# Local attention: the blocks of the transposed weights in another order, so that constant zero columns are neither copied nor multiplied

## The chip, the cores and the metric

One core of a Trainium2 chip runs the whole program. The metric is the device time of one execution in microseconds (us); below it stands the median of several executions. TensorE multiplies (PE in the profile, its weight loads PEld), VectorE (DVE), ScalarE (ACT) and GpSimd (POOL) work beside it, and SyncE (SP) issues transfers.

## What is computed

Six blocks are applied one after the other to x of shape 4 x 256 x 256 (batch, tokens, features), each with a residual: cross attention over 4096 context tokens, causal attention with a convolution, a local transformer of six layers, a second cross attention, gated linear attention and a mixture of experts. The change acts on the third, and rearranges the second. Each layer of the third has 16 heads of 64 features and attends inside a window:

```
def local_attention(q, k, v):            # n = 256 tokens, WINDOW = 64
    ...
    mask = (it < jb) | (it > jb + w) | (jb == -1)
    sim = jnp.einsum('bhwie,bhwje->bhwij', bq, bk2) * QK_SCALE
    sim = jnp.where(mask, -jnp.finfo(sim.dtype).max, sim)
    attn = jax.nn.softmax(sim, -1)
    out = jnp.einsum('bhwij,bhwje->bhwie', attn, bv2)
```

So token i sees the tokens i-64 to i. Tokens 192 to 255 see none of the tokens 0 to 127.

## The kernel before

The six blocks run in turn, each as one stage with a program for each engine. Local (L1365 on) is the stage of the local transformer. It has 24 jobs, one for each layer l and batch b, and a plan that is written out by hand: TABLE and LOADS give each step a tick, a job has 24 ticks, and all steps are sorted by tick. Every engine walks through this one sorted plan in order, so that an engine that waits holds up everything that it has behind the wait. The attention of a job is laid over the projections of the next one (HEADS = 24.18 ticks later): projections (L1911, 128x512 passes in fp32r), rotary embedding on VectorE (L1775 to L1779), the squares on ScalarE (L1686), transposes of q and k (L1948), then the heads, the output projection (L1976), a normalisation (L1836 to L1856), the transposes of its result (L1989), the feed-forward's matmuls (L1998 and L2008). At the change of a layer, the next layer's projection weights are split into a high and a low part by ScalarE (L1679) and VectorE (L1748).

The heads are the work of the class Attention, which the second block (Conv) uses too. A head n passes through four kinds of steps, and every step comes to all engines:

- front: two score matmuls (L1017). Query tile 0 (tokens 0 to 127) meets keys 0 to 127, and query tile 1 (tokens 128 to 255) meets keys 64 to 255, 192 of them, because the constructor gets skip = 64. VectorE adds the mask and takes the smallest value (L1053), and ScalarE takes the exponential (L1078). Both write p, 384 columns wide: columns 0 to 127 are query tile 0, columns 128 to 191 are zeros that were set once, columns 192 to 383 are query tile 1 on keys 64 to 255.
- divide: the reciprocal of the sum (L1058), and the products on VectorE (L1061) and GpSimd (L1068).
- turn: three transposes of 128x128 (L1026) into one PSUM bank, and one copy of 384 columns to pt by ScalarE (L1084). The blocks of pt are, in order: queries 0 to 127 on keys 0 to 127; queries 128 to 255 on keys 0 to 127; queries 128 to 255 on keys 128 to 255. In the second block the columns of queries 192 to 255 are zeros.
- apply: for two heads at once (at_once = 2, one in the rows 0 to 63 of the PSUM bank and one in the rows 64 to 127), the values of the first key tile times 256 columns of pt, then the values of the second key tile times 128 columns, added to the right half (L1037). Each of these float32 matmuls appears in the trace as two passes, so that an apply is 8 passes. ScalarE copies the result away (L1530).

Over the 24 jobs there are 384 heads and 192 applies. In Conv skip is 0 and at_once is 4; there are 128 heads there.

Of the kernel before, what the change touches and what calls it, by code (L numbers as in the profile page):

```python
# [7 lines left out]
F32 = mybir.dt.float32  # L8
# [5 lines left out]
P = 128  # L14
# [11 lines left out]
class Flow:  # L26


    def __init__(self, sem, step):
        self.sem, self.step, self.base, self.n = sem, step, 0, 0  # L30
# [934 lines left out]
class Attention:  # L965
# [8 lines left out]
    def __init__(self, c, name, ctx, banks, n_pt, at_once, rounds, skip):  # L974
        nc = c.nc
        self.c, self.at_once, self.rounds = c, at_once, rounds
        self.s_banks, self.t_banks, self.o_bank = banks
        self.keys, self.first, self.off = (P, 2 * P - skip), (0, skip), (0, P)
        self.place = (0, P + skip)
        self.width, self.n_pt, self.step = sum(self.keys), n_pt, P // at_once  # L980
        self.p = ctx.enter_context(nc.sbuf_tensor(f"{name}_p", [P, 5, 3 * P], F32))
        self.pt = ctx.enter_context(nc.sbuf_tensor(f"{name}_pt", [P, n_pt, 3 * P], F32))
        self.stat = ctx.enter_context(nc.sbuf_tensor(f"{name}_stat", [P, 5, 4, 2], F32))
        f = c.flow
        self.s_full, self.low_done, self.exp_done = f("at_s_full"), f("at_low_done"), f("at_exp_done")
        self.div_dve, self.div_pool = f("at_div_dve"), f("at_div_pool")
        self.t_full, self.t_out = f("at_t_full"), f("at_t_out")
        self.pv_done, self.o_out = f("at_pv_done"), f("at_o_out")
# [21 lines left out]
    def pe_step(self, pe, on, st, step):  # L1010
        kind, n, b, h = step
        NS = len(self.s_banks)
        if kind == "front":
            s = self.s_banks[n % NS]
            on.wait_ge(self.low_done, 2 * (n - NS) + 2)
            for q in range(2):
                mm = pe.matmul(s[:, self.off[q]:self.off[q] + self.keys[q]], st.q_of(b, h, q),  # L1017
                               st.k_of(b, h, self.first[q], self.keys[q]), start=True, stop=True)
            mm.then_inc(*self.s_full.one())
        elif kind == "turn":  # L1020
            on.wait_ge(self.div_dve, 2 * n + 2)
            on.wait_ge(self.div_pool, n + 1)
            on.wait_ge(self.t_out, n - 1)
            for i in range(3):
                at = slice(i * P, (i + 1) * P)
                tr = pe.transpose(self.t_banks[n % 2][:, at], self.p[:, n % 5, at], self.c.ident[:, :])  # L1026
            tr.then_inc(*self.t_full.one())
        elif kind == "apply":
            heads, call = h, n // self.at_once
            round_ = call % self.rounds  # L1030
            on.wait_ge(self.t_out, n + len(heads))
            if round_ == 0:
                on.wait_ge(self.o_out, call // self.rounds)
            for first, cols, keys, kt in ((True, slice(0, 2 * P), slice(0, 2 * P), 0),
                                          (False, slice(P, 2 * P), slice(2 * P, 3 * P), 1)):
                for j, head in enumerate(heads):
                    mm = pe.matmul(self.o_bank[self.step * j:self.step * j + self.step, cols],  # L1037
                                   st.v_of(b, kt, head), self.pt[:, (n + j) % self.n_pt, keys],
                                   start=first and round_ == 0,
                                   stop=not first and round_ == self.rounds - 1)  # L1040
            mm.then_inc(*self.pv_done.one())

    def dve_step(self, dve, on, st, step):
# [27 lines left out]
    def act_step(self, act, on, st, step):  # L1071
        kind, n, b, h = step
        t3 = self.stat[:, n % 5, :, :]
        if kind == "front":
            for q in range(2):
                low = self.p[:, n % 5, self.place[q]:self.place[q] + self.keys[q]]
                on.wait_ge(self.low_done, 2 * n + q + 1)
                act.activation(low, low, ACT.Exp, bias=t3[:, 0, q:q + 1], scale=-1.0,  # L1078
                               accum_out=t3[:, 2, q:q + 1]).then_inc(*self.exp_done.one())
        elif kind == "turn":  # L1080
            on.wait_ge(self.t_full, n + 1)
            if n >= self.n_pt:
                on.wait_ge(self.pv_done, (n - self.n_pt) // self.at_once + 1)
            act.activation(self.pt[:, n % self.n_pt, :], self.t_banks[n % 2][:, 0:3 * P],  # L1084
                           ACT.Copy).then_inc(*self.t_out.one())
        elif kind == "apply":
            call = n // self.at_once
            if call % self.rounds == self.rounds - 1:
                on.wait_ge(self.pv_done, call + 1)
                st.keep(act, on, n, b, h, self.o_bank)  # L1090
# [2049 lines left out]
```

## Time and profile before

| | |
|---|---|
| median of 3 runs | 4458.15 us (4455.14 to 4465.23) |
| profiled execution | 4470.84 us |
| its span in the trace | 4469.0 us |
| mean granted TensorE clock | 0.968 |
| stage of the local transformer | about 1290 to 2965 us of the span |

The profiled execution is one execution of its own and lies 12.7 us above the median. The trace gives, for each engine, when each instruction began and how long it took; matmuls overlap in their pipeline, so their durations add up to more than the time that they hold TensorE.

### The profile page before, as it was taken

What the parts mean: (1) busy time and instruction counts of PE and PEld (TensorE: products, weight loads), DVE (VectorE), ACT (ScalarE), POOL (GpSimd) and SP (SyncE); (2) the same over time, 40 slices, a digit from 0 to 9 for tenths busy, and PEclk for the clock granted to TensorE, in tenths of its full rate; (3) what the DMA queues carried; (4) which work ended last, traced back from release to release, by engine and by line L of the source; (5) the groups of instructions that cost most, each with busy time, mean ns of one, the idle gap of its engine ahead of it and who ended that gap; (6) DMA issues with size and microseconds to landing.
All of it is one profiled execution on the core that took longest, in us unless ns stands there. A gap on an engine that the chain in (4) does not pass through costs nothing. (4 is left out here: it accounts for less than half of the span.)

```text
span 4469.0 us, 83297 instructions
## 1 busy us (share of the span) xinstructions
PE 4072.7 (91%) x30320; PEld 2916.0 (65%) x30320; DVE 3121.6 (70%) x7923; ACT 2814.7 (63%) x5769; POOL 1809.5 (40%) x1862
## 2 busy tenths in 40 slices
PE   6899999898979999999999999968999999977898
PEld 4555555555757888888878888845555555545677
DVE  5677777776777767667677676546777777767645
ACT  3666666667976777777677676715666666654322
POOL 3322222212566565555556555413223222201544
PEclk8999999999989999999999999989999999988999
DMA  6655556545020100001100101036556555512265
GB/s 153 133 105 108 103 98 115 109 64 203 10 76 5 34 31 30 24 29 32 39 22 25 38 22 38 15 84 138 114 101 111 102 106 106 100 27 70 83 177 190
DMA packets 208206, 354.14 MB, mean 79 GB/s; under 512 B 26927, under 2 KB 110564, under 8 KB 205745
## 3 DMA queue, kind: packets, MB, share of 16 engines
q1 hardware_dynamic: 200217, 338.42, 34.0%
q0 software_dynamic: 7584, 10.39, 0.7%
q8 instruction: 246, 4.03, 0.4%
q14 instruction: 159, 1.30, 0.1%
HBM read 257.48 MB, written 114.98 MB: 83 GB/s over the span
## 5 line engine op out<-in xcount | busy, mean ns | idle before, releaser
L754 DVE TENSOR_REDUCE xa_m_part<-xa_ring 128x1 f32<-128x512 f32 x2048 | 1318.4, 685 | 501.6 <-PE xa_ring L907 487.1
L676 ACT ACTIVATE xa_ex<-xa_sc 128x1024 f32<-128x1024 f32 x1024 | 991.4, 1022 | 120.6 <-PE xa_sc L893 105.4
L907 PE MATMUL xa_ring<-xa_ks,xa_q_base 48*128 48x512 f32 x2048 | 521.4, 500 | 166.9 <-DVE xa_m_part L754 131.6
L921 PE MATMUL xa_pv<-xa_ex,xa_vs 128*17 128x256 f32 x8192 | 553.1, 388 | 1.7 <-issue 1.7
L1068 POOL TENSOR_SCALAR lt_p<-lt_p,lt_stat 128x192 f32<-128x192 f32 x384 | 354.6, 924 | 456.0 <-DVE lt_stat L1058 455.4
L907 PEld LDWEIGHTS xa_ring<-xa_ks,xa_q_base 48*128 48x128 f32 x2048 | 202.6, 186 | 497.5 <-DVE xa_m_part L754 431.0
L1911 PE MATMUL lt_bank<-lt_wp,lt_xt 128*128 128x512 f32 x1728 | 465.6, 411 | 13.6 <-DVE lt_wp L1748 6.0
L893 PE MATMUL xa_sc<-xa_q_base,xa_ks 50*128 50x256 f32 x4096 | 423.7, 302 | 27.9 <-ACT xa_k L648 4.5
L893 PEld LDWEIGHTS xa_sc<-xa_q_base,xa_ks 50*128 50x128 f32 x4096 | 347.7, 188 | 122.3 <-ACT xa_vs L663 24.6
L1078 ACT ACTIVATE lt_p<-lt_p,lt_stat 128x128 f32<-128x128 f32 (+1 forms) x768 | 321.8, 420 | 157.4 <-DVE lt_stat L1053 154.8
L1911 PEld LDWEIGHTS lt_bank<-lt_wp,lt_xt 128*128 128x128 f32 x1728 | 315.2, 192 | 78.7 <-DVE lt_xt L1741 9.1
L1625 POOL TENSOR_TENSOR lt_r_qk<-lt_r_qk,lt_t_rot 128x512 f32<-128x512 f32 x192 | 267.5, 1394 | 203.9 <-DVE lt_t_rot L1779 198.2
L1053 DVE CUSTOM_DVE_ANT_0 lt_p<-lt_bank,lt_mask,lt_rq 128x128 f32<-128x128 f32 (+1 forms) x768 | 260.9, 376 | 123.7 <-PE lt_bank L1017 120.6
L598 POOL CAST xa_kp<-xa_k 128x512 fp32r<-128x512 f32 (+1 forms) x144 | 86.2, 599 | 625.2 <-ACT xa_k L656 286.7
L921 PEld LDWEIGHTS xa_pv<-xa_ex,xa_vs 128*17 128x17 f32 x8192 | 189.7, 97 | 201.3 <-issue 63.7
L1632 POOL TENSOR_TENSOR lt_nrm<-lt_nrm,minus_half 128x16 f32<-128x16 f32 x96 | 281.9, 2936 | 21.6 <-DVE lt_nrm L1796 18.7
L1998 PE MATMUL lt_bank<-lt_ft,lt_w 128*128 128x256 f32 x1152 | 267.7, 383 | 9.3 <-DVE lt_ft L1856 5.9
L1686 ACT ACTIVATE lt_t_sq<-lt_bank 128x512 f32<-128x512 f32 x192 | 114.7, 598 | 226.2 <-DVE lt_t_rot L1779 226.2
L1998 PEld LDWEIGHTS lt_bank<-lt_ft,lt_w 128*128 128x128 f32 x1152 | 214.7, 191 | 41.5 <-issue 12.6
L610 POOL TENSOR_SCALAR xa_m_neg<-xa_m_blk 128x8 f32<-128x8 f32 x128 | 29.7, 232 | 520.1 <-DVE xa_m_blk L765 515.1
L876 PE MATMUL xa_sc<-xa_wp,xa_cxp 128*128 128x256 f32 x1536 | 213.7, 289 | 0.0
L862 PE MATMUL xa_sc<-xa_cxp,xa_wp 128*128 128x512 f32 x744 | 211.4, 421 | 0.0
(325 smaller groups left out, 7943.0 us busy)
## 6 DMA issues: line engine op xcount, KB each, us to landing
xa_ks<-keys SPq DMA_DIRECT2D x372, 256.0 KB
keys<-xa_kp SPq DMA_DIRECT2D x128, 512.0 KB, 3.8
xa_cx<-in_ctx_t SPq DMA_DIRECT2D x64, 512.0 KB
lt_u<-in_lt_wqkv SPq DMA_DIRECT2D x54, 256.0 KB
places<-in_moe_blank SPq DMA_DIRECT2D x47, 258.0 KB, 9.6
moe_xs<-places SPq DMA_DIRECT2D x47, 258.0 KB
lt_w<-in_lt_w SPq DMA_DIRECT2D x6, 1536.0 KB
xa_q_base<-xa_m_rows SPq DMA_DIRECT2D x512, 2.0 KB
```

What stands on the lines that cost most here:

```text
L676: act.activation(x.ex[:, n % x.NE, :, :], x.sc[n % 2][:, :, :], ACT.Exp).then_inc(*x.ex_done.one())
L754: dve.tensor_reduce(x.m_part[:, i % 2, qt, h, ch:ch + 1], x.bank(n + odd), AX.X, ALU.max).then_inc(*x.dve_out.one())
L893: mm = pe.matmul(x.sc[n % 2][:, 2 * odd + pair, :], x.ks[unit % x.NU][rows, 2 * (g % 2) + pair, kt * P:(kt + 1) * P], x.q_base[rows, 2 * g ...
L907: pe.matmul(x.bank(n + odd), x.q_base[rows, pair, b * S + qt * P:b * S + (qt + 1) * P], x.ks[unit % x.NU][rows, pair % 4, ch * 512:(ch + 1 ...
L921: mm = pe.matmul(x.pv[32 * j:32 * j + x.VW, :], x.vs[:, i % x.NV, kt, 4 * g + j, :], x.ex[:, n % x.NE, 2 * (j % 2) + j // 2, :], start=(kt ...
L1053: dve.tensor_tensor_reduce(self.p[:, n % 5, to], s[:, at], st.mask[:, at], st.minus_scale(b, h, q), -NEG, ALU.add, ALU.min, t3[:, 0, q:q + ...
L1068: pool.tensor_scalar(sv, sv, self.stat[:, n % 5, 3, 1:2], None, ALU.mult).then_inc(*self.div_pool.one())
L1078: act.activation(low, low, ACT.Exp, bias=t3[:, 0, q:q + 1], scale=-1.0, accum_out=t3[:, 2, q:q + 1]).then_inc(*self.exp_done.one())
L1625: pool.tensor_tensor(out, out, self.t_rot[:, t, :], ALU.add).then_inc(*self.rot_add.one())
L1632: pool.tensor_tensor(n[:, 2, :], n[:, 1, :], c.minus_half[:, 0:H], ALU.pow).then_inc(*self.rnorm.one())
L1911: mm = pe.matmul(bank[:, :], self.xt[:, par, xpart, k, tile * P:(tile + 1) * P], self.wp[:, wpart, sec, k, half * 512:half * 512 + 512], s ...
L1998: mm = pe.matmul(bank[:, gate * S:(gate + 1) * S], self.w1[:, k, gate * FFP + m * P:gate * FFP + (m + 1) * P], self.ft[:, k, :], start=(k ...
```

## The change

The three transposes write to other places of their PSUM bank. The block of queries 128 to 255 on keys 128 to 255 comes first, that of queries 0 to 127 on keys 0 to 127 second, and that of queries 128 to 255 on keys 0 to 127 last, so that the 64 columns of zeros lie at the end. The copy to pt ends ahead of them (320 columns in place of 384), and the matmul on the first key tile takes the 192 columns that are left in place of 256. The output columns 192 to 255 are then written for the first time by the matmul on the second key tile, which has start=False. In Conv the widths stay as they were and only the order of the blocks is another.

```
+        self.both, self.whole = 2 * P - skip, skip == 0
-        self.pt = ctx.enter_context(nc.sbuf_tensor(f"{name}_pt", [P, n_pt, 3 * P], F32))
+        self.pt = ctx.enter_context(nc.sbuf_tensor(f"{name}_pt", [P, n_pt, 3 * P - skip], F32))
...
-            for i in range(3):
-                at = slice(i * P, (i + 1) * P)
-                tr = pe.transpose(self.t_banks[n % 2][:, at], self.p[:, n % 5, at], self.c.ident[:, :])
+            for i, to in enumerate((P, 2 * P, 0)):
+                tr = pe.transpose(self.t_banks[n % 2][:, to:to + P], self.p[:, n % 5, i * P:(i + 1) * P],
+                                  self.c.ident[:, :])
...
-            for first, cols, keys, kt in ((True, slice(0, 2 * P), slice(0, 2 * P), 0),
-                                          (False, slice(P, 2 * P), slice(2 * P, 3 * P), 1)):
+            for first, cols, keys, kt in ((True, slice(0, self.both), slice(P, P + self.both), 0),
+                                          (False, slice(P, 2 * P), slice(0, P), 1)):
...
-                                   stop=not first and round_ == self.rounds - 1)
+                                   stop=not first and round_ == self.rounds - 1,
+                                   skip_group_check=not self.whole)
...
-            act.activation(self.pt[:, n % self.n_pt, :], self.t_banks[n % 2][:, 0:3 * P],
+            act.activation(self.pt[:, n % self.n_pt, :], self.t_banks[n % 2][:, 0:self.width],
                            ACT.Copy).then_inc(*self.t_out.one())
```

## Rows read from the trace of the kernel before

**Rows 1.** The page's busy time of each engine over the whole span.
```profile
PE 4072.7 (91%) x30320; PEld 2916.0 (65%) x30320; DVE 3121.6 (70%) x7923; ACT 2814.7 (63%) x5769; POOL 1809.5 (40%) x1862
```

**Rows 2.** Busy time of each engine in the stage, then in its steady part.
```profile
core 0: us, PE busy (x) PEld busy (x) DVE busy (x) ACT busy (x) POOL busy (x), PEclk, DMA share, GB/s
1290.00:2965.00 1675.00, 1611.37 (x9479) 1335.81 (x9480) 1143.59 (x3899) 1164.85 (x3073) 933.15 (x747) 0.98 0.10 31
1345.00:2920.00 1575.00, 1542.62 (x9210) 1282.83 (x9211) 1083.20 (x3763) 1129.76 (x3019) 902.44 (x727) 1.00 0.09 27
```

**Rows 3.** Who waited for whom, 1345 to 2920 us: total, times, longest (us).
```profile
DVE lt_p L1053 <- PE lt_bank L1017: 116.5, 82, 3.9
DVE lt_r_qk L1775 <- PE lt_bank L1911: 78.2, 80, 2.2
...
PE lt_bank L1948 <- DVE lt_r_qk L1805: 14.6, 7, 2.7
...
PE lt_bank L1998 <- DVE lt_ft L1856: 4.8, 15, 0.6
PE lt_bank L1998 <- issue: 3.4, 6, 0.6
...
PEld lt_bank L1037 <- ACT lt_pt L1084: 1.5, 3, 0.8
```

**Rows 4.** Groups by line and shape, 1345 to 2920 us: busy us, mean ns.
```profile
L1084 ACT ACTIVATE lt_pt<-lt_bank 128x384 f32<-128x384 f32 x384 | 183.1, 477 | 1.8
L1037 PE MATMUL lt_bank<-lt_pt,lt_v 128*64 128x256 f32 x768 | 125.3, 405 | 0.8 <-ACT lt_pt L1084 0.8
L1017 PE MATMUL lt_bank<-lt_kt,lt_q_odd 128*128 128x192 f32 x382 | 95.1, 331 | 0.0
L1037 PE MATMUL lt_bank<-lt_pt,lt_v 128*64 128x128 f32 x768 | 74.6, 273 | 0.0
L1530 ACT ACTIVATE lt_ot<-lt_bank 128x256 f32<-128x256 f32 x192 | 69.7, 363 | 1.0 <-PE lt_bank L1037 1.0
```

**Rows 5.** Timeline of TensorE around one apply: start us, us.
```profile
1902.56 0.60 PE L1948 MATMUL lt_bank<-ident,lt_r_qk 128*128 128x128 f32 x4
1903.00 0.71 PE L1017 MATMUL lt_bank<-lt_kt,lt_q_odd 128*128 128x128 f32 x4
1903.55 0.49 PE L1026 MATMUL lt_bank<-ident,lt_p 128*128 128x128 f32 x3
...
1904.52 0.87 PE L1037 MATMUL lt_bank<-lt_pt,lt_v 128*64 128x256 f32 x8
1905.32 0.33 PE L1026 MATMUL lt_bank<-ident,lt_p 128*128 128x128 f32 x1
```

**Rows 6.** Timeline of TensorE, one long run of 256-column passes.
```profile
2923.07 7.07 PE L1976 MATMUL lt_bank<-lt_wo,lt_ot 128*128 128x256 f32 x32
```

**Rows 7.** Timelines of VectorE and TensorE ahead of a job's first L1998.
```profile
1638.79 0.69 DVE L1775 TENSOR_TENSOR lt_r_qk<-lt_bank,lt_tab 128x512 f32<-128x512 f32 x1 [1.48 <-PE lt_bank L1911]
...
1642.78 0.98 DVE L1856 TENSOR_SCALAR lt_ft<-lt_bank,lt_lnc 128x256 f32<-128x256 f32 x2
...
1641.95 0.87 PE L1037 MATMUL lt_bank<-lt_pt,lt_v 128*64 128x256 f32 x8
...
1643.91 3.69 PE L1998 MATMUL lt_bank<-lt_ft,lt_w 128*128 128x256 f32 x16 [0.61 <-DVE lt_ft L1856]
```

**Rows 8.** The same two engines where a layer ends.
```profile
2297.40 0.69 DVE L1775 TENSOR_TENSOR lt_r_qk<-lt_bank,lt_tab 128x512 f32<-128x512 f32 x1 [1.06 <-PE lt_bank L1911]
...
2317.18 2.98 DVE L1748 TENSOR_TENSOR lt_wp<-lt_u,lt_wp 128x512 fp32r<-128x512 f32 x3 [0.28 <-ACT lt_wp L1679]
...
2315.53 0.87 PE L1037 MATMUL lt_bank<-lt_pt,lt_v 128*64 128x256 f32 x8
...
2322.95 0.66 PE L1948 MATMUL lt_bank<-ident,lt_r_qk 128*128 128x128 f32 x4 [2.21 <-DVE lt_r_qk L1805]
```

**Rows 9.** VectorE and the others between the first and last row above.
```profile
2297.40:2322.95 25.55, 22.60 (x136) 17.87 (x135) 24.96 (x74) 19.56 (x54) 18.58 (x14) 1.00 0.14 44
```

**Rows 10.** Windows of 14 us at two layers' ends (PEclk is the clock's share).
```profile
1777.00:1791.00 14.00, 11.63 (x58) 9.84 (x57) 8.75 (x24) 9.80 (x23) 4.30 (x4) 0.88 0.01 2
2317.00:2331.00 14.00, 11.16 (x63) 9.11 (x64) 9.64 (x27) 10.61 (x28) 4.85 (x5) 1.00 0.01 1
```

**Rows 11.** The same wait of TensorE at three more layers' ends.
```profile
1783.09 0.93 PE L1948 MATMUL lt_bank<-ident,lt_r_qk 128*128 128x128 f32 x4 [2.19 <-DVE lt_r_qk L1805]
2053.04 1.12 PE L1948 MATMUL lt_bank<-ident,lt_r_qk 128*128 128x128 f32 x4 [2.22 <-DVE lt_r_qk L1805]
2592.05 0.92 PE L1948 MATMUL lt_bank<-ident,lt_r_qk 128*128 128x128 f32 x4 [2.20 <-DVE lt_r_qk L1805]
```

## The prediction

> **What bounds the kernel now.** I read the page's busy times first: TensorE is busy for 91% of the span, VectorE for 70%, ScalarE for 63% [rows 1]. Those are means over six stages with different limits, so the next view is the windows. The change touches only the stage of the local transformer, 1290 to 2965 us. In its steady part, 1345 to 2920 us, TensorE is busy for 1542.6 of 1575 us (98%), at a granted clock of 1.00, while ScalarE has 1129.8 us of work (72%), VectorE 1083.2 (69%) and GpSimd 902.4 (57%) [rows 2]. Durations of matmuls overlap, so 98% could still hide pauses. The waits settle that: the largest that TensorE has for another engine is 14.6 us, for the scaled keys, then 4.8 and 3.4 us at the first matmul of the feed-forward. VectorE waits for TensorE 116.5 us at the scores and 78.2 us at the projections [rows 3]. TensorE sets the pace and the others follow it. So the question is what the change takes out of TensorE's stream, and how much of that TensorE then spends waiting.
>
> **The wide matmuls of apply.** An apply has 8 passes of TensorE: 4 of 256 columns and 4 of 128, 768 of each over the stage [rows 4], which are 192 applies. Durations say little about how long a pass holds the engine; starts do. 32 passes of 256 columns take 7.07 us from the first start to the last end. The last alone lasts about 0.38 us, so there are 31 steps in 6.69 us, 216 ns each [rows 6]. Passes of 128 columns start every 0.44 / 4 = 110 ns. The scores, two of 128 and two of 192, take 1903.55 - 1903.00 = 0.55 us, which leaves (0.55 - 0.22) / 2 = 165 ns for one of 192 [rows 5]. So 256 to 192 columns is worth 216 - 165 = 51 ns; by the lengths of the same passes it is (405 - 273) / 2 = 66 ns for 64 columns, where 405 holds a start-up share that won't shrink, and by the spacing of 256 and 128 it is (216 - 110) / 2 = 53 ns. I take 53.
>
> The two heads go to different rows of the bank. One apply takes 1905.32 - 1904.52 = 0.80 us up to the next transposes [rows 5]; four 256-column and four 128-column passes one after the other would take 1.3 us. So the two heads' passes run side by side, and the 8 passes are 4 pairs, of which 2 are narrowed. The saving is 2 x 53 = 106 ns for an apply and 192 x 0.106 = 20.4 us for the stage. The other two pairs, the start-up and the step back to full-width transposes stay as they are. No pass is added. That the last 64 output columns are first written by a matmul with start=False costs nothing that I can find: it has the same columns and the same number of passes. No row shows such a write; between 0 and a step of 110 ns for an apply (the nearest pass) it could cost 0 to 21 us, and I take 0, since it replaces a write of the same size to the same bank.
>
> The Trainium skill (TensorE: Matmul & The Clock Gate, "Back-to-back issue gap") puts the spacing of warm matmuls at columns / 2.4 plus 2.5 ns, which would be 109 ns for 256 columns. The trace has twice that for these float32 passes [rows 6], and the trace decides. By the page 64 columns are worth 27 ns, and the sum above would be an estimated 10.2 us.
>
> **The copy.** The copy to pt takes 477 ns for 384 columns, and ScalarE's copy of 256 columns out of the same kind of bank takes 363 [rows 4]: 0.89 ns for a column, 57 ns for 64. Over 384 heads ScalarE gets 21.9 us back, of its 1129.8. It has 28% idle, and TensorE waited for pt for 1.5 us in all [rows 3], because the apply comes several steps after the turn in the plan. I cost it at nothing; the cover is TensorE's own work between turn and apply. The upper bound is what TensorE's waits on it hold, 1.5 us, and if more of the late scores hang on ScalarE's queue, about as much again: 3 us.
>
> **The order of the transposes.** Three transposes of the same size into the same bank, and the copy waits for the last one either way: 0. In Conv the widths are unchanged too, so 0 for its 128 heads. The buffer pt gets smaller, and no transfer or wait is added or moved.
>
> **What is given back in waits.** The shortening acts where TensorE leads. Where VectorE leads over a stretch, TensorE only comes earlier to a wait that ends at the same time. There are two such places.
> - Ahead of each job's first L1998. VectorE last waited for TensorE at 1638.79 us. From there it works without a pause to L1856 at 1642.78, whose end lets TensorE go on at 1643.91 after 0.61 us of waiting. One apply, at 1641.95, lies within [rows 7]. That saving of 0.106 us is lost. The wait shows 15 + 6 = 21 times [rows 3]: 2.2 us.
> - Where a layer ends. VectorE has the splits of the next weights on top: from 2297.40 to 2322.95 us it is busy for 24.96 of 25.55 us, and TensorE waits 2.21 us at the end of it [rows 8, 9]. In this stretch I count three applies, of which the last, at 2315.53, belongs to the first place. Two more by 0.106 us by five ends of a layer: 1.1 us.
>
> What is late next: steps that now have less slack than up to 0.9 us a job (8 applies by 0.106) will begin to show as waits. The rows don't give the slack; the bounds are 0 and, if every job had one more such place with half its applies ahead of it, 24 x 0.4 = 10 us. VectorE is idle for 31% of the time and mostly waits for TensorE, so I stay near the low end, 1 us.
>
> **Sum.** 20.4 - 2.2 - 1.1 - 1.0 = 16.1 us. The profiled execution took 4470.8 us and should come to 4454.7. It lies 12.7 us above the median of the runs; I take the same saving off the median: 4458.2 - 16.1 = 4442 us. About 0.2% (9 us) is what a measurement of this kernel can tell from no change.
>
> **The rivals.**
> - *The forecast* (0.67): TensorE keeps the lead, 13 to 20 us are saved, 4438 to 4445 us.
> - *More* (0.10): ScalarE's shorter queue brings scores and tiles forward where TensorE waited. To 20.4 come the 3 us above: 4435 us. For it: ScalarE is the second busiest engine. Against: almost no wait of TensorE ends on it [rows 3].
> - *A narrower pass gives less than its columns* (0.09): by the page's gap, named above, or because the pass in each apply that loads its weights uncovered hides part of the stream. With half the saving on the pairs, 20.4 / 2 = 10.2, less half of the 3.3 given back: 8.6 us, 4450 us. Against it: the scores' 192 columns at 165 ns [rows 5], a like pass of full width.
> - *Given back in waits* (0.10): the 10 us bound holds rather than 1. 20.4 - 3.3 - 10 = 7 us, 4451 us; with VectorE leading for more of the job, down to nothing, 4458. For it: VectorE had no slack in the stretch of rows 9. Against: outside such stretches it waits for TensorE in each job [rows 3].
> - *Slower, by the clock* (0.04): after some ends of a layer the clock is halved for a while; the window from 1777 us has 0.88 of it, so (1 - 0.88) x 14 / 0.5 = 3.4 us at 1.2 GHz, while that from 2317 us has 1.00 [rows 10]. TensorE had waited 2.2 us before both. Layers with the fall last 269.95 us (1783.09 to 2053.04), one without 269.10 (2322.95 to 2592.05) [rows 8, 11], so a fall costs 0.85 us there, and 1.7 us (half of 3.4) in a stretch without slack. If longer waits brought it in after each of the 21 + 5 waits, that is 26 x 1.7 = 44 us against 16 saved: 28 us slower, 4486 us. It decides from about 15 more falls on, as 25 us would be needed to be 0.2% slower. Against it: the waits grow by only 0.1 to 0.3 us, and 0.6 us waits leave the clock at 1.00 now.
>
> **How the numbers follow.** The forecast and *more* are faster by over 0.2%, and so is near half of *a narrower pass gives less*, as 8.6 us is just under the 9 us bound: 0.67 + 0.10 + 0.04 = 0.81, plus 0.01 of the waits. The rest of these two is no change: 0.14. Slower keeps 0.04. The range goes from *more* with the spread of a median, 4432, to the upper bounds of the two small-gain cases, 4452; what it leaves out is most of the waits case below 6 us and the clock.
>
> **What would show it.** Right: L1037's wide passes listed as 128x192, near 330 ns; an apply that takes 0.69 us in place of 0.80; the copy as 128x320 near 420 ns; ScalarE's busy time in the stage down by 22 us; the job's period down by 0.6 to 0.8 us; TensorE's waits at L1998 and L1948 larger by 3 to 4 us in all; all other stages unchanged. Wrong: an apply that still takes 0.75 us or more (a pass is worth less than its columns), or an apply of 0.69 us with waits of TensorE that grew by 10 us or more (VectorE leads), or windows with a clock under 1.00 inside jobs (the clock).

## The result and the profile after

The changed kernel takes 4444.5 us (median of 20 runs, 4427.9 to 4459.0), the kernel before 4459.7 us (20 runs, 4450.3 to 4470.5). The ratio is 0.9965, with an interval of 0.9955 to 0.9974: 15.6 us faster, between 11.6 and 20.1 (the medians are 15.2 us apart). The forecast was 16.1 us. On two more chips the changed kernel came out at 0.996 (0.9946 to 0.9974) and 0.9964 (0.995 to 0.9979) of the kernel before.

The page of the changed kernel, its busy times, beside [rows 1]:

```profile
PE 4047.2 (91%) x30320; PEld 2906.1 (65%) x30320; DVE 3123.8 (70%) x7923; ACT 2795.1 (63%) x5769; POOL 1811.3 (41%) x1862
```

The same number of instructions, 25.5 us less on TensorE, 19.6 us less on ScalarE, VectorE and GpSimd as before. The windows of the stage in the changed kernel, its whole length and its steady part (us, busy and count for each engine, TensorE's clock, DMA), answer to [rows 2]:

```profile
core 0: us, PE busy (x) PEld busy (x) DVE busy (x) ACT busy (x) POOL busy (x), PEclk, DMA share, GB/s
1297.50:2945.80 1648.30, 1581.17 (x9458) 1326.21 (x9459) 1138.83 (x3883) 1142.37 (x3069) 933.05 (x745) 0.99 0.10 31
1351.00:2907.00 1556.00, 1518.13 (x9214) 1276.44 (x9213) 1084.82 (x3765) 1110.08 (x3020) 903.75 (x727) 1.00 0.09 28
```

and the window of the same length of work in the kernel before, from the stage's first matmul to its last:

```profile
1291.40:2958.90 1667.50, 1607.52 (x9459) 1333.49 (x9460) 1137.68 (x3882) 1162.29 (x3068) 931.75 (x745) 0.98 0.10 31
```

The stage is 19.2 us shorter. TensorE is still busy for 98% of the steady part, so it is still the bound. The spans of the two profiled executions differ by more, 4469.0 to 4443.8 = 25.2 us. From its first matmul to its last, the stage of the experts took 383.1 us in the one and 370.8 in the other, and the first cross attention 1035.6 and 1041.4, with the same instructions: that part is not the change's. The experts' stage takes from 369.4 to 383.1 us in ten of the fourteen profiles, with the change and without it.

The groups by line and shape in the steady part of the changed kernel (busy us, mean ns), beside [rows 4]:

```profile
L1086 ACT ACTIVATE lt_pt<-lt_bank 128x320 f32<-128x320 f32 x384 | 162.8, 424 | 1.8
L1038 PE MATMUL lt_bank<-lt_pt,lt_v 128*64 128x192 f32 x768 | 104.8, 352 | 0.6 <-ACT lt_pt L1086 0.5
L1038 PE MATMUL lt_bank<-lt_pt,lt_v 128*64 128x128 f32 x768 | 74.6, 273 | 0.0
L1532 ACT ACTIVATE lt_ot<-lt_bank 128x256 f32<-128x256 f32 x192 | 69.7, 363 | 0.9 <-PE lt_bank L1038 0.9
```

The wide passes went from 405 to 352 ns, 53 less; the passes of 128 columns stayed at 273 ns and the copy of the result at 363. The copy went from 477 to 424 ns. TensorE's timeline of the changed kernel where [rows 7] were read:

```profile
1644.63 0.76 PE L1038 MATMUL lt_bank<-lt_pt,lt_v 128*64 128x192 f32 x8
1645.33 0.55 PE L1026 MATMUL lt_bank<-ident,lt_p 128*128 128x128 f32 x3
1646.60 3.69 PE L2000 MATMUL lt_bank<-lt_ft,lt_w 128*128 128x256 f32 x16 [0.72 <-DVE lt_ft L1858]
```

An apply takes 1645.33 - 1644.63 = 0.70 us in place of 0.80 [rows 5]. Over all 192 applies the median from an apply's first start to the next pass behind it went from 802 to 695 ns, 107 less. The wait behind the apply shown is 0.72 us in place of 0.61 [rows 7]: what this apply saved, TensorE waits.

Three waits in the steady part (total us, times, longest), first of the kernel before, then of the changed one: TensorE's for the low part of the features (lt_xt), its wait for the gate of the feed-forward (lt_u), and that of its weight loads ahead of the feed-forward:

```profile
PE lt_bank L1911 <- DVE lt_xt L1741: 2.8, 5, 0.6
PE lt_bank L1948 <- DVE lt_u L1869: 2.3, 3, 1.2
...
PEld lt_bank L1998 <- issue: 12.6, 21, 0.8
```

```profile
PE lt_bank L1913 <- DVE lt_xt L1743: 4.0, 5, 0.8
PE lt_bank L1950 <- DVE lt_u L1871: 3.8, 6, 1.2
...
PEld lt_bank L2000 <- issue: 14.9, 21, 0.9
```

Last, the wait at two layers' ends in the changed kernel, beside [rows 11], and windows of 14 us at them, beside [rows 10]:

```profile
1784.55 0.66 PE L1950 MATMUL lt_bank<-ident,lt_r_qk 128*128 128x128 f32 x4 [2.22 <-DVE lt_r_qk L1807]
2051.06 0.66 PE L1950 MATMUL lt_bank<-ident,lt_r_qk 128*128 128x128 f32 x4 [2.22 <-DVE lt_r_qk L1807]
```

```profile
1780.00:1794.00 14.00, 11.26 (x66) 9.26 (x65) 8.72 (x28) 10.54 (x26) 4.65 (x4) 1.00 0.01 2
2313.00:2327.00 14.00, 11.26 (x67) 9.24 (x66) 8.79 (x28) 10.54 (x26) 4.64 (x5) 1.00 0.00 1
```

A layer takes 2051.06 - 1784.55 = 266.5 us. In the kernel before it was 269.1 with the full clock and 269.95 with a stretch at the half clock [rows 8, 11]. So the change is worth 2.6 us a layer, and the clock's fall, which this execution doesn't show at any layer's end, 0.85 us. The stage has six layers, so an estimate of the change's own part of it is 6 x 2.6 = 15.6 us. That this is the figure of the timed runs to the tenth is chance, as their interval reaches about 4 us to each side. The rest of the 19.2 us goes with the clock: the execution before has such stretches at three layers' ends and one in the first layer, the one after none. Each lasts 3.4 us.

### The profile page after: what moved, and what is told of

Same layout as the page of the kernel before. It is cut to its first block and busy times, and to the rows that moved or that the text cites. A ratio compares the mean times of both kernels' runs of the same rounds, so it can differ in the third digit from the quotient of the medians.

```text
span 4443.8 us, 83297 instructions
## 1 busy us (share of the span) xinstructions
PE 4047.2 (91%) x30320; PEld 2906.1 (65%) x30320; DVE 3123.8 (70%) x7923; ACT 2795.1 (63%) x5769; POOL 1811.3 (41%) x1862
## 5 line engine op out<-in xcount | busy, mean ns | idle before, releaser
L2000 PE MATMUL lt_bank<-lt_ft,lt_w 128*128 128x256 f32 x1152 | 267.2, 382 | 11.6 <-DVE lt_ft L1858 7.5
L2000 PEld LDWEIGHTS lt_bank<-lt_ft,lt_w 128*128 128x128 f32 x1152 | 214.3, 191 | 43.7 <-issue 14.9
```

Source lines behind the costliest of these rows:

```text
L2000: mm = pe.matmul(bank[:, gate * S:(gate + 1) * S], self.w1[:, k, gate * FFP + m * P:gate * FFP + (m + 1) * P], self.ft[:, k, :], start=(k ...
```

## The experiments

Theory A: TensorE's stream sets the pace, so the gain is the columns of the wide passes, less what is lost in waits where VectorE leads. The rivals are that the order of the blocks (B) or ScalarE's shorter copy (C) gives a part of it, that a pass has a floor or VectorE soon takes the lead (D), and two on the waits (E) and on the array's rows (F, G).

Single timed runs of one kernel scatter by 9 to 31 us, and the runs came in three groups, each on one chip, with the kernel before at 4466.8, 4435.1 and 4458.1 us (chips 1 to 3 below). So each run's profile is read for two lengths that the rest of the kernel doesn't touch: the stage, from its first matmul to its last, and one layer, from a layer's first apply to the next layer's (the second to the fifth were read). "Falls" counts the stretches at the half clock in the stage's steady part, the first layer included. The edits below are against the changed kernel, that of before_ft_first against the kernel before; lines are shortened with "...".

| kernel | ratio to before (interval) | stage us | falls | layer us, without / with a fall |
|---|---|---|---|---|
| before (profile of the prediction) | 1 | 1667.6 | 4 | 269.1 / 269.9 |
| changed (profile of the result) | 0.9965 (0.9955 to 0.9974) | 1648.4 | 0 | 266.5 / - |
| after_again, chip 1 | 0.996 (0.9946 to 0.9974) | 1651.0 | 3 | 266.5 / 267.3 |
| order_only, chip 1 | 1.0003 (0.999 to 1.0016) | 1667.8 | 4 | 269.1 / 270.0 |
| copy_only, chip 1 | 0.9998 (0.9987 to 1.0009) | 1667.7 | 4 | 269.1 / 269.9 |
| mm_only, chip 1 | 0.9957 (0.9945 to 0.997) | 1650.7 | 2 | 266.6 / - |
| mm_128, chip 2 | 0.9928 (0.9908 to 0.9948) | 1638.2 | 4 | 264.0 / 265.0 |
| ft_first, chip 2 | 0.9933 (0.9913 to 0.9953) | 1646.1 | 5 | - / 266.2 |
| before_ft_first, chip 2 | 0.9991 (0.9976 to 1.0005) | 1659.9 | 4 | 267.8 / 268.7 |
| half_rows, chip 2 | 1.0135 (1.0114 to 1.0157) | 1729.4 | 4 | 279.7 / 280.8 |
| after_2, chip 3 | 0.9964 (0.995 to 0.9979) | 1650.8 | 2 | 266.5 / - |
| ft_first_2, chip 3 | 0.9952 (0.9939 to 0.9966) | 1644.1 | 5 | - / 266.0 |
| splits_late, chip 3 | 0.9956 (0.9944 to 0.9969) | 1652.5 | 2 | 266.1 / - |
| ft_splits, chip 3 | 0.9958 (0.9943 to 0.9972) | 1647.0 | 6 | - / 266.2 |

### The change itself again: after_again and after_2

> The changed kernel as it is, beside the others on one chip. Both theories expect what the study's result gave: ratio 0.9965, about 15 to 16 us under the kernel before.

> The changed kernel once more, beside the three below on one chip: ratio about 0.996 to the kernel before, 32 applies (one layer) in 266.5 us where the clock stays full and 267.4 where it is halved for a while.

The layers are the same to 0.1 us in all three profiles where the clock stays full. A fall at a layer's end adds 0.8 us (267.3 and 266.5), and between 0.8 and 1.1 us in the other kernels of the table. Two of them in the stage's first layer add 2.5 us (259.1 in both of these profiles, 256.6 in that of the result, which has none).

### One part at a time: order_only, copy_only, mm_only

> Only the order of the blocks of the transposed weights is changed; the copy stays at 384 columns and the wide passes at 256. Theory A (TensorE's stream sets the pace, and only its columns count): no change, within 3 us of the kernel before; an apply still takes 0.80 us. Rival B (part of the gain comes from the new places of the blocks in the banks): 3 to 8 us faster.

```
-        self.both, self.whole = 2 * P - skip, skip == 0
+        self.both, self.whole = 2 * P, True
-        self.pt = ... [P, n_pt, 3 * P - skip]
+        self.pt = ... [P, n_pt, 3 * P]
-            act.activation(self.pt[...], self.t_banks[n % 2][:, 0:self.width], ...)
+            act.activation(self.pt[...], self.t_banks[n % 2][:, 0:3 * P], ...)
```

No change: 1.0003, and the stage is within 0.2 us of that before, with as many falls. Rival B is out.

> New order, copy of 320 columns, passes still 256 wide (the last 64 columns of the buffer are set to zero once). ScalarE gets about 21 us of work less. Theory A: 0 to 2 us faster, because TensorE hardly ever waits for ScalarE. Rival C (ScalarE, the second busiest engine, shares the pace): 5 to 10 us faster, a third to a half of the gain.

```
-        self.both, self.whole = 2 * P - skip, skip == 0
+        self.both, self.whole = 2 * P, True
-        self.pt = ... [P, n_pt, 3 * P - skip]
+        self.pt = ... [P, n_pt, 3 * P]
-            act.activation(self.pt[:, n % self.n_pt, :], ...)
+            act.activation(self.pt[:, n % self.n_pt, 0:self.width], ...)
+                dve.memset(self.at.pt[:, :, 3 * P - WINDOW:3 * P], 0.0)
```

The groups of copy_only show the two halves apart, the short copy and the wide passes:

```profile
L1086 ACT ACTIVATE lt_pt<-lt_bank 128x320 f32<-128x320 f32 x380 | 161.2, 424 | 1.8
L1038 PE MATMUL lt_bank<-lt_pt,lt_v 128*64 128x256 f32 x760 | 124.0, 405 | 0.1
```

ScalarE has its 53 ns a head, and the stage is as long as before: 1667.7 us, ratio 0.9998. The copy is worth nothing here. The interval of the ratio alone reaches to 5.8 us faster; it is the stage that rules rival C out.

> New order, passes 192 wide, copy still of 384 columns. Theory A: the whole gain, 14 to 17 us faster than the kernel before, within 2 us of the changed kernel. Rival C: 5 to 10 us short of it. The apply should take 0.69 us in place of 0.80 either way.

```
-        self.pt = ... [P, n_pt, 3 * P - skip]
+        self.pt = ... [P, n_pt, 3 * P]
-            act.activation(self.pt[...], self.t_banks[n % 2][:, 0:self.width], ...)
+            act.activation(self.pt[...], self.t_banks[n % 2][:, 0:3 * P], ...)
```

The groups of mm_only:

```profile
L1086 ACT ACTIVATE lt_pt<-lt_bank 128x384 f32<-128x384 f32 x384 | 183.5, 478 | 1.8
L1038 PE MATMUL lt_bank<-lt_pt,lt_v 128*64 128x192 f32 x768 | 104.8, 352 | 0.8 <-ACT lt_pt L1086 0.8
```

0.9957, and a layer of 266.6 us against 266.5 of the whole change. All of the gain is the narrow passes: the applies of mm_only take 695 ns, as in the changed kernel, and those of copy_only 802, as before.

One row needs care. The weight loads of apply seem to wait for the copy much more in the changed kernel than in mm_only. Waits of TensorE's weight loads (total us, times, longest), the changed kernel:

```profile
PEld lt_bank L1038 <- issue: 33.0, 146, 0.3
...
PEld lt_bank L1038 <- ACT lt_pt L1086: 11.1, 46, 0.8
```

In the kernel before, and in mm_only, the same two read 42.7 and 1.5 us; in copy_only they read 33.2 and 10.8. The sums are 44.1, 44.2, 44.2 and 44.0: the pause ahead of an apply is the same, and only its label moves when the copy is shorter.

### The same step once more: mm_128

> The changed kernel with the first key tile's passes 128 wide in place of 192; it leaves out the products of queries 128 to 191 with keys 0 to 127. Theory A (time goes by columns, less what is given back where VectorE leads): the same step once more, another 13 to 16 us, 28 to 32 us faster than the kernel before, an apply of 0.58 us, and TensorE's wait ahead of each job's first feed-forward matmul 0.1 us longer again. Rival D (passes have a floor set by their weight loads or VectorE takes the lead): under 8 us more than the change gave.

```
-        self.both, self.whole = 2 * P - skip, skip == 0
+        self.both, self.whole = 2 * P - 2 * skip, skip == 0
```

This kernel leaves out products that the result needs; it is there for its time alone. TensorE's timeline of mm_128 at the same place:

```profile
1637.69 0.66 PE L1038 MATMUL lt_bank<-lt_pt,lt_v 128*64 128x128 f32 x8
1638.28 0.55 PE L1026 MATMUL lt_bank<-ident,lt_p 128*128 128x128 f32 x3
1639.70 3.69 PE L2000 MATMUL lt_bank<-lt_ft,lt_w 128*128 128x256 f32 x16 [0.87 <-DVE lt_ft L1858]
```

An apply takes 0.59 us (median 588 ns, again 107 less), the wait 0.87, and a layer 264.0 us: 2.5 us less again, where 32 applies by 0.106 would be 3.4. Six layers make that 15 us; the ratio, 0.9928, says about 16 us more than the change's 0.9965, within wide intervals. The step repeats with nearly the same loss, so down to passes of 128 columns there is no floor and rival D is out.

### Who leads ahead of the feed-forward: ft_first and before_ft_first

> The changed kernel with one step of the plan moved: the second half of the first projection comes behind the transposes of the normalised features instead of ahead of them, so that VectorE's scaling of them isn't behind three rotary operations and TensorE has six passes to do meanwhile. Theory A (VectorE's queue order makes the wait of 0.34 to 0.9 us in nearly every job, and a part of the saving is lost in it): the wait ahead of the first feed-forward matmul goes, and the kernel gains 8 to 14 us over the changed one. Rival E (the wait only moves to the next step behind VectorE): under 4 us.

> The kernel before with the same step moved. Theory A: 6 to 11 us faster than the kernel before (its waits there are 2 us shorter in all than in the changed kernel), so that narrow passes on top of it are worth 17 to 19 us in place of 15.5, since that apply's saving isn't lost. Rival E: no change, and narrow passes are worth 15 to 16 us as before.

```
-    TABLE = ((-5.23, "proj", 0, 0, 0), (-4.15, "proj", 0, 0, 1), ...
+    TABLE = ((-5.23, "proj", 0, 0, 0), (-3.4, "proj", 0, 0, 1), ...
```

The ratios, 0.9933 and 0.9991, would make the narrow passes worth 26 us on top of the moved step. The profiles contradict that: a layer is 267.8 us without a fall, and 266.2 with one, so about 265.35 without (by 0.85 for a fall): 2.45 us, not more than the 2.6 of the unmoved plan. Where both have a fall it is 268.7 against 266.2, again 2.5 us. Theory A had expected the narrow passes to be worth more there; they aren't, and rival E had that right. On the moved step itself it was right by the profile: a layer takes 267.8 us in place of 269.1, and the stage, with four falls in each, 7.7 us less. The timed runs, 4 us with an interval that reaches from 11 us faster to 2 slower, don't settle that. Next, ft_first beside the changed kernel on one chip.

> ft_first once more, now on the same chip as the changed kernel. From its profile (a layer in 266.2 us with the halved clock at each layer's end, against 266.5 without it in the changed kernel) the theory now is that the moved step gains 1.2 us a layer and a longer wait at the layer's end takes 0.85 back through the clock: 2 to 7 us faster than the changed kernel. Rival: the 12 us that the ratios of different chips seemed to show.

TensorE's timeline of ft_first_2, ahead of the feed-forward and at a layer's end:

```profile
1635.83 0.55 PE L1026 MATMUL lt_bank<-ident,lt_p 128*128 128x128 f32 x3
1636.21 3.62 PE L2000 MATMUL lt_bank<-lt_ft,lt_w 128*128 128x256 f32 x16
...
1641.36 0.66 PE L1950 MATMUL lt_bank<-ident,lt_r_qk 128*128 128x128 f32 x4 [0.16 <-DVE lt_u L1871]
```

```profile
1774.10 1.02 PE L1950 MATMUL lt_bank<-ident,lt_r_qk 128*128 128x128 f32 x4 [2.84 <-DVE lt_r_qk L1807]
...
2040.10 0.79 PE L1950 MATMUL lt_bank<-ident,lt_r_qk 128*128 128x128 f32 x4 [2.84 <-DVE lt_r_qk L1807]
```

and its windows at two layers' ends:

```profile
1771.00:1785.00 14.00, 11.16 (x61) 9.69 (x60) 7.19 (x26) 10.78 (x26) 5.20 (x4) 0.88 0.01 2
2037.00:2051.00 14.00, 11.16 (x62) 9.66 (x61) 7.18 (x26) 10.83 (x27) 5.25 (x4) 0.88 0.01 1
```

The wait ahead of L2000 is gone, as theory A had it, so VectorE's order of work did cause it. But a wait of 0.16 us stands five microseconds later, that at the layer's end grew from 2.22 to 2.84 us (VectorE itself now waits 1.18 us there for ScalarE's part of the splits, L1681, in place of 0.28), and the clock now falls at four of the five layers' ends (all five in ft_first). A layer takes 266.0 us in place of 266.5. On the one chip the medians are 4438.4 and 4441.7 us, with ratios whose intervals overlap. Those 3 us are in line with the second expectation, and far from the 8 to 14 us of the first; there rival E was nearer. The 12 us between the ratios of chips 1 and 2 didn't come again, and the stages show no such difference.

### Who leads where a layer ends: splits_late and ft_splits

> The changed kernel with VectorE's four splits of the next layer's key weights (2.8 us) behind the scaling of the keys instead of ahead of it. Theory A (the queue order of VectorE makes the wait of 2.4 us at each layer's end, and what narrow passes save in that stretch is lost there): the wait falls under 0.8 us, a layer takes 264.5 to 265.5 us, no halved clock, 5 to 9 us faster than the changed kernel. Rival (the splits only move the wait behind themselves, to the gates of the feed-forward): a layer still takes over 266 us.

```
-             (20.73, "split", 3, (1, 0)), (20.85, "split", 3, (1, 1)), ...
+             (21.4, "split", 3, (1, 0)), (21.5, "split", 3, (1, 1)), ...
```

TensorE's timeline of splits_late where a layer ends:

```profile
2315.64 0.60 PE L1950 MATMUL lt_bank<-ident,lt_r_qk 128*128 128x128 f32 x4
...
2319.72 0.66 PE L1950 MATMUL lt_bank<-ident,lt_r_qk 128*128 128x128 f32 x4 [2.60 <-DVE lt_u L1871]
```

The first transposes no longer wait, the next ones wait 2.60 us, now for the gate of the feed-forward (L1871). A layer is 266.1 us, so the rival was right that the wait moves. But VectorE's queue isn't what holds the gate. VectorE's timeline of splits_late, the last split and the gate:

```profile
2316.57 0.68 DVE L1750 TENSOR_TENSOR lt_wp<-lt_gl,lt_wp 128x512 fp32r<-128x512 f32 x1
2317.17 0.67 DVE L1791 TENSOR_REDUCE lt_nrm<-lt_t_sq 128x8 f32<-128x512 f32 x1
2319.18 0.88 DVE L1871 SCALAR_TENSOR_TENSOR lt_u<-lt_bank,lt_ffc,lt_gl 128x256 f32<-128x256 f32 x2 [1.34 <-ACT lt_gl L1721]
```

VectorE is idle for 1.34 us ahead of the gate, at each of the five layers' ends, and waits for ScalarE, whose own step (L1721) waits in the program for the splits (L1715). ScalarE begins it at 2317.31, 0.06 us after the last split has ended, with a table load of 1.28 us, and only then computes what the gate needs. So the chain that took over is split, ScalarE's table load and gate, VectorE's gate. No run takes the table load out of it.

> Both moves of the plan in the changed kernel. Theory A: the two places where VectorE leads are both relieved, a layer takes 263 to 264.5 us, 10 to 16 us faster than the changed kernel, about 0.993 of the kernel before. Rival (a third place takes over): under 8 us.

Both moves together give 266.2 us a layer with a fall in each, a stage of 1647.0 us and a ratio of 0.9958. That is no better than ft_first_2 alone, and the rival was right. TensorE waits 3.15 us for the gate at each layer's end, and ahead of it VectorE waits for ScalarE as in splits_late (1.34 us at each of the five ends). No version that computes the same is clearly faster than the changed kernel in the timed runs; by its stage ft_first_2 is, by 4 to 7 us.

### The zeros in the transposes: half_rows

> The changed kernel with the transpose of queries 128 to 255 on keys 0 to 127 cut to queries 128 to 191, from 64 partitions, 64 columns instead of 128. Theory F (a pass costs by its columns, whichever rows it uses): 384 x 55 ns = 21 us less of TensorE, 15 to 20 us faster than the changed kernel. Rival G (each change between 64 and 128 rows costs about what the change of column tiles costs around an apply, 0.09 us on either side): 384 x (0.18 - 0.055) = 48 us more, 35 to 50 us slower than the changed kernel.

```
             for i, to in enumerate((P, 2 * P, 0)):
+                rows = P if i != 1 or self.whole else P // 2
-                tr = pe.transpose(self.t_banks[n % 2][:, to:to + P], self.p[:, n % 5, i * P:(i + 1) * P],
-                                  self.c.ident[:, :])
+                tr = pe.transpose(self.t_banks[n % 2][:, to:to + rows], self.p[0:rows, n % 5, i * P:(i + 1) * P],
+                                  self.c.ident[0:rows, 0:rows])
```

TensorE's timeline of half_rows:

```profile
1908.61 0.73 PE L1027 MATMUL lt_bank<-ident,lt_p 128*128 128x128 f32 x3
1909.18 1.04 PE L1951 MATMUL lt_bank<-ident,lt_r_qk 128*128 128x128 f32 x8
```

The three transposes hold TensorE for 0.57 us, where three full ones take 3 x 0.11 = 0.33 [rows 5]. By columns they should take 0.275, so going to 64 rows and back costs 0.57 - 0.275 = 0.295 us. It isn't the same on both sides. By the starts of the single passes in this stretch (1908.607, 1908.810, 1909.012 and 1909.176 us), the 64-row transpose comes 0.20 us after a full one, 0.09 more than between full ones. The next full one comes again 0.20 us later, 0.15 more than 64 columns take, and the pass behind that 0.165 us later, 0.055 more than behind full ones. So it is 0.09 us on the way in and 0.20 on the way back. In the weight loads the pause shows ahead of the 64-row one:

```profile
1908.45 0.14 PEld L1027 LDWEIGHTS lt_bank<-ident,lt_p 128*128 128x128 f32 x1
1908.81 0.34 PEld L1027 LDWEIGHTS lt_bank<-ident,lt_p 64*128 64x128 f32 x2 [0.22 <-issue]
```

A layer is 13.2 us longer than in the changed kernel, 206 ns for each of its 64 heads, and the stage about 78 us longer than in after_again and after_2. Rival G was right in kind and too low, with 35 to 50 us: its 0.09 us holds on the way in and not on the way back. Theory F is out.

## Why the prediction was right

- **What bounds the kernel.** Shown. Taking 20 us off TensorE's stream alone (mm_only) gave the whole gain, taking 20 us off ScalarE alone (copy_only) nothing.
- **53 ns for 64 columns of a pass.** Measured 405 - 352 = 53 ns, and 107 ns for an apply against 106, in the change and once more in mm_128. The alternative from lengths, 66 ns, was wrong for the reason given, the start-up share. The same share made me forecast "near 330 ns" for the mean of the narrow passes; it is 352, since half of them still carry it: they last about 377 ns and the others about 326. The Trainium skill's gap (TensorE: Matmul & The Clock Gate, "Back-to-back issue gap"), which the page gives for a single matmul by itself and not for a stream, would have given 27 ns; neither the change nor mm_128 shows it.
- **A write that starts with start=False costs nothing.** Nothing of it is visible: an apply got shorter by 107 ns with 64 columns first written so, and by 107 more with 128 (mm_128), where the columns alone say 106 each.
- **The copy.** 53 ns instead of the forecast 57, so ScalarE got back about 20 us of the 22 forecast, and that was worth nothing, shown by copy_only. The order of blocks is worth nothing too, shown by order_only.
- **Ahead of the feed-forward, 2.2 us lost.** The waits of the weight loads there grew from 12.6 to 14.9 us over the same 21 times: 2.3 us. mm_128 adds 2.6 more (17.5 us).
- **Where a layer ends, 1.1 us lost.** The size was right and the place wrong. The wait at the end of the stretch stayed at 2.2 us [rows 8]. The loss is at the wait for the low part of the features (L1741), inside the stretch, which went from 2.8 to 4.0 us over five times, 1.2 us. In the timeline of rows 8 it is this one:

```profile
2310.67 1.66 PE L1911 MATMUL lt_bank<-lt_wp,lt_xt 128*128 128x512 f32 x6 [0.56 <-DVE lt_xt L1741]
```

In the changed kernel it is 0.80 us, 0.24 more: the two applies that the prediction counted, at 2300.55 and 2307.36, both stand ahead of it.
- **1 us for new waits.** A layer lost 32 x 0.106 - 2.6 = 0.8 us, so 4.8 us are given back in six, against 4.3 forecast. The new waits stand at the gate (L1869), from 2.3 us in three times to 3.8 in six. That the 1 us nearly held is partly luck: it was a choice between bounds of 0 and 10, and no row gave the slack.
- **The clock.** It didn't speak against the change: the falls are at the same kind of place, at three of the five layers' ends in the one profile of the kernel before, and at none, two and one in the three of the changed kernel. ft_first showed that the rival has something to it all the same: with waits of 2.8 us instead of 2.2 the fall comes at nearly every layer's end. Over the fourteen profiles, a fall goes with the wait at 19 of 45 layers' ends where it is 2.0 to 2.2 us, at 4 of 10 where it is 2.6 or 2.7 (splits_late and before_ft_first), and at 14 of 15 where it is 2.8 or 3.15. The price is 0.8 to 1.1 us where a kernel has layers of both kinds, near the 0.85 forecast. Whether the longer wait is the cause was not tested by itself.

## What to carry to other kernels

In a stage where one engine has no pause, only its own work counts: 20 us of an engine at 72% were worth nothing, 20 us of the one at 98% were worth 16. The missing fifth can be forecast (here 4.3 us, of which 1 us was a guess, for about 4.8) by walking back from each wait of the leading engine to the point where the other engine last waited for it, and counting the shortened instructions between. Removing such a wait by reordering gave less than its length in the three plans tried on the changed kernel, since another wait grew, in two of them by way of a third engine; and when a gain is 0.3%, the length of one layer in a profile tells kernels apart that twenty timed runs hardly do.

## What the runs showed of the hardware

- Going from 128 to 64 rows of the array cost 0.09 us and going back 0.20, and turned a saving of 55 ns a head into a loss of 206 (half_rows).
- Narrowing a pair of float32 passes by 64 columns shortened an apply by the same 53 ns a pair from 256 to 192 columns and from 192 to 128 (802, 695 and 588 ns an apply).
- The same wait of 2.2 us at a layer's end is sometimes followed by 3.4 us at half the clock (1.2 GHz) and sometimes not, in the same kernel: at none, two and one of the five ends in three profiles of the changed kernel.
- The kernel before ran at 4435 to 4467 us by the chip. The stage of the experts took 383.1 us in the profile of before, 354.4 on chip 2 with the same code of that stage (before_ft_first), and in all 348.4 to 354.4 us in the four profiles from chip 2 against 369.4 to 383.1 in the ten others. Nothing here shows why.
